# Plain x for the last layer's experts, a gate per token on VectorE, and a new order of all engines

## The reference, cut to what matters

```
logits = xf @ gate_w.T                        # n x 8
w, sel = top_k(logits, 2); w = softmax(w)
w_full = zeros(n, 8).at[arange(n)[:, None], sel].add(w)
expert_out = einsum('nc,edc->ned', xf, expert_w)
out = einsum('ne,ned->nd', w_full, expert_out)
x = layernorm(x + out)
```

## Time and profile before

| | |
|---|---|
| median of 3 runs | 1725.61 us (1722.67 to 1727.79) |
| the profiled execution, its own time | 1721.39 us |
| its span, first to last instruction | 1719.6 us |
| TensorE busy | 85% of the span, granted clock 0.958 of full on average |
| VectorE busy | 75% |
| ScalarE busy | 53% |
| GpSimd busy | 51% |
| DMA | 214.26 MB |

### The profile page before, as it was taken

The page is one execution under the profiler, slowest core; times in us unless marked ns, Lnnn a source line. Parts: engine busy times, 40 slices in busy tenths (PEclk is TensorE's granted clock), DMA queues, the critical chain, the costliest instruction groups (busy, mean ns, idle before and its releaser), DMA issues.

```text
span 1719.6 us, 36166 instructions
## 1 busy us (share of the span) xinstructions
PE 1465.4 (85%) x12928; PEld 1134.0 (66%) x12928; DVE 1297.0 (75%) x3466; ACT 913.0 (53%) x1868; POOL 882.3 (51%) x772
## 2 busy tenths in 40 slices
PE   2799889999999999999999999999999999985534
PEld 1567666776777767777777767677777767664423
DVE  2466888888888888788888888888888888875552
ACT  1356555566655555566655555566565556563310
POOL 0013565555556665555556665555555655555532
PEclk8799999999999999999999999999999999998765
DMA  4223344444444434544444334444444334433330
GB/s 120 98 93 95 113 131 126 152 144 131 138 132 134 128 115 138 152 148 128 139 136 132 126 114 139 152 130 146 124 147 125 119 126 145 148 87 108 83 111 31
DMA packets 88983, 214.26 MB, mean 125 GB/s; under 512 B 10499, under 2 KB 67075, under 8 KB 67459
## 3 DMA queue, kind: packets, MB, share of 16 engines
q1 hardware_dynamic: 88804, 211.95, 40.9%
HBM read 185.97 MB, written 25.69 MB: 123 GB/s over the span
## 4 chain that ended last, share of the span: by engine, by line
PE 39%; DVE 24%; issue 18%; POOL 11%; ACT 3%; DMA 3%; SPq 1%; DVEq 0%; POOLq 0%; ACTq 0%
POOL wb L1059 8%; PE b L508 7%; PE bPV L529 6%; DVE mx L993 5%; PE bS L546 4%; PE b L567 4%; PE bTU L558 4%; PE bTU L559 3%; POOL prod L1068 2%; DVE wb L962 2%; DVE wb L911 2%; PE bS L549 2%; DVE mneg L1036 2%; DVE gat L975 1%; DVE wb L969 1%
## 5 line engine op out<-in xcount | busy, mean ns | idle before, releaser
L1059 POOL TENSOR_TENSOR wb<-wb 128x1024 f32<-128x1024 f32 x64 | 150.6, 2354 | 498.0 <-DVE wb L911 498.0
L993 DVE TENSOR_REDUCE mx<-bS 128x2 f32<-128x512 f32 x512 | 338.5, 683 | 57.2 <-PE bS L549 55.7
L1068 POOL TENSOR_TENSOR prod<-kC,qC 128x512 f32<-128x512 f32 x256 | 349.1, 1399 | 37.2 <-ACT kC L670 37.2
L701 ACT ACTIVATE P<-bTU 128x512 f32<-128x512 f32 x512 | 277.0, 607 | 106.0 <-PE bTU L481 79.1
L1093 POOL TENSOR_TENSOR h<-ub,gBcb 128x256 f32<-128x256 f32 x256 | 184.0, 730 | 188.1 <-DVE ub L1006 153.5
L546 PE MATMUL bS<-stack 96*128 96x256 bf16 x1024 | 217.8, 280 | 35.3 <-DVE mx L993 14.8
L478 PE MATMUL bTU<-stack 97*128 97x256 bf16 x1024 | 227.3, 275 | 5.5 <-ACT P L701 2.5
L481 PE MATMUL bTU<-dist,identh 128*128 128x128 f16 x1024 | 206.5, 220 | 0.0
L558 PE MATMUL bTU<-x1T,w 128*128 128x256 f32 x576 | 184.1, 402 | 24.6 <-DVE h L1006 24.6
L549 PE MATMUL bS<-dist,identh 128*128 128x128 f16 x1024 | 197.1, 223 | 0.0
L710 ACT ACTIVATE sil<-bTU,b 128x256 f32<-128x256 f32 x288 | 130.1, 475 | 104.6 <-PE bTU L559 56.4
(11 more groups left out here) (159 smaller groups left out, 2781.7 us busy)
## 6 DMA issues: line engine op xcount, KB each, us to landing
wb<-d_w SPq DMA_DIRECT2D x64, 1024.0 KB, 7.8
stack<-d_parts SPq DMA_DIRECT2D x192, 192.0 KB
gBcb<-d_cB SPq DMA_DIRECT2D x32, 1024.0 KB, 4.8
gDcb<-d_cD SPq DMA_DIRECT2D x32, 1024.0 KB, 4.7
d_parts<-parts SPq DMA_DIRECT2D x96, 128.0 KB, 5.2
d_w<-wT SPq DMA_DIRECT2D x32, 256.0 KB, 2.1
xT<-in_xT SPq DMA_DIRECT2D x32, 128.0 KB, 4.7
x<-in_x SPq DMA_DIRECT2D x32, 128.0 KB, 2.1
```

Of the source, the lines that this page charges most:

```text
L701: act_f(P[k % 8][:].rearrange("p a b -> p (a b)"), bTU[turn_bank("ST", k)][:], ACT.Exp).then_inc(actA2.done("exp", k), 1)
L993: v.tensor_reduce(mx[:, :, k], bS[k % 2][:].rearrange("p (a b) -> p a b", a=TT), op=ALU.max, axis=AX.X).then_inc(dveA1.done("max", k), 1)
L1059: tt_(pv[:, 8 * n:8 * n + 4, :], pv[:, 8 * n:8 * n + 4, :], pv[:, 8 * n + 4:8 * n + 8, :], ALU.add).then_inc(poolC2.done("add", n), 1)
L1068: tt_(prod[:, 2 * p:2 * p + 2, :], shifted(kC, p), qC[:].unsqueeze(1).to_broadcast([128, 2, T]), ALU.mult).then_inc(poolC1.done("prod", p), 1)
```

## The change

Six things change together.

1. Stage D. TensorE multiplies the plain x of 128 tokens with two experts' weights side by side (256 columns) into a bank of the three that ST and `ab` use in turn: `D.y`, four steps. VectorE adds each expert's output, times the token's gate as a scalar of its partition, to x: `D.acc`, 16 instructions of 128x128 that read PSUM and SBUF. `D.xs`, `D2.y`, `D2.res`, the transpose, copy, store and broadcast of D's gates go. `D2.mom` keeps the moments of the norm.
2. The maxima are written negated in bf16 by the reduction itself; `M.neg` goes.
3. Ranks: a difference and a comparison with a table of the smallest number replace two comparisons, a product and an add.
4. Roots: two steps of a tuned iteration (seven instructions) in place of three (nine).
5. Distances: q is divided by its head's slope and the exponential multiplies by it, so that one fp16 table holds the plain distances of every head; the second product of odd heads in ST goes, and the constant shrinks from 1024 KB to one head's 32 KB.
6. All five orders are new.

```diff
 ORDER = {
     "pe": """
-        A1.qk A1.v B2.z D2.y.0 A2.ST.0 D2.y.1 A2.ST.1 A2.ST.2 A2.ST.3 A2.ST.4 A2.ST.5 A2.ST.6 A2.PV.0 A2.ST.7
-        A2.ST.8 B.xT A2.ST.9 A2.PV.1 D.xT B.lg D.lg A2.ST.10 A2.ST.11 A2.ST.12 A2.ST.13 A2.PV.2 C1.xT A2.ST.14 B.cT
-        A2.ST.15 B.ab.0 A2.PV.3 C1.qk A1.S.0 A1.S.1 B.ab.1 A3.pT A1.S.2 C1.vg B.ab.2 A1.S.3 A1.S.4 B.ab.3 A1.S.5
-        D.cT B.ab.4 A1.S.6 A3.aT C2.out A1.S.7 A1.S.8 B.ab.5 A3.out A1.S.9 A1.S.10 C1.sc A1.S.11 A1.S.12 C1.scT
-        B.ab.6 A1.S.13 A1.S.14 B.ab.7 B.z A1.S.15 C1.wT B.ab.8 M.mT""",
+        A1.qk B2.z A1.v A2.ST.0 A2.ST.1 A2.ST.2 A2.ST.3 A2.ST.4 A2.ST.5 A2.PV.0 A2.ST.6 A2.ST.7 B.xT A2.ST.8 A2.ST.9
+        A2.PV.1 A2.ST.10 C1.xT A2.ST.11 D.xT A2.ST.12 B.lg D.lg A2.ST.13 A2.ST.14 C1.qk A2.ST.15 A2.PV.2 D.y.0 D.y.1
+        A2.PV.3 D.y.2 B.cT C1.vg B.ab.0 A1.S.0 A1.S.1 B.ab.1 A3.pT A1.S.2 A1.S.3 B.ab.2 A1.S.4 A1.S.5 B.ab.3 A1.S.6
+        A1.S.7 C2.out B.ab.4 A1.S.8 A1.S.9 C1.sc A1.S.10 B.ab.5 C1.scT A1.S.11 B.ab.6 B.ab.7 A1.S.12 B.z A1.S.13
+        C1.wT A1.S.14 A3.aT A1.S.15 B.ab.8 A3.out M.mT D.y.3""",
     "act": """
-        A1.qk A2.exp.0 A2.exp.1 A2.exp.2 A2.exp.3 A2.exp.4 A2.exp.5 A2.exp.6 A3n.nm A2.exp.7 C2n.nm B.xT B2.nm D.xT
-        A2.exp.8 A2.exp.9 D2.nm A2.exp.10 A2.exp.11 A2.exp.12 G.ge A2.exp.13 C1.xT A2.exp.14 A2.exp.15 B.cT C1.qk
-        A3.cp B.ab.0 B.ab.1 C1.vg D.cT B.ab.2 B.ab.3 B.ab.4 A3.aT C1.sc B.ab.5 B.ab.6 C1.exp B.ab.7 C1.wT B.ab.8
-        M.mT""",
+        A1.qk A2.exp.0 A2.exp.1 A2.exp.2 A2.exp.3 A2.exp.4 A3n.nm B2.nm A2.exp.5 A2.exp.6 A2.exp.7 A2.exp.8 A2.exp.9
+        B.xT C2n.nm A2.exp.10 D.xT C1.xT A2.exp.11 A2.exp.12 A2.exp.13 G.ge A2.exp.14 D2.nm C1.qk A2.exp.15 B.cT
+        A3.cp B.ab.0 B.ab.1 B.ab.2 C1.vg B.ab.3 B.ab.4 C1.sc B.ab.5 C1.exp B.ab.6 C1.wT A3.aT B.ab.7 M.mT B.ab.8""",
     "dve": """
-        A1.rest A1.v A1.mid A1.lo B2.res D2.res N.root.0 N.root.1 N.root.2 N.root.3 C2.pv.0 C2.pv.1 C2.pv.2 C2.pv.3
-        G.rank C2.pv.4 G.weigh C2.pv.5 C2.pv.6 C2.pv.7 C2.add.0 A1.max.0 A1.max.1 C2.add.1 A1.max.2 C2.add.2 A3.rec
-        B.wu.0 C2.gt A1.max.3 B.wu.1 A1.max.4 A3.num A1.max.5 A1.max.6 B.wu.2 A1.max.7 A1.max.8 C2.res A1.max.9
-        B.wu.3 A1.max.10 B.wu.4 A1.max.11 A1.max.12 C1.mx B.wu.5 B.wu.6 A1.max.13 A1.max.14 C1.sum B.wu.7 A1.max.15
-        M.neg A3.res B.wu.8""",
+        B2.res D2.mom A1.rest N.root.0 A1.v N.root.1 A1.mid N.root.2 A1.lo N.root.3 C2.pv.0 C2.pv.1 C2.pv.2 C2.pv.3
+        C2.pv.4 C2.pv.5 C2.pv.6 G.rank C2.pv.7 G.weigh D.acc.0 C2.add.0 D.acc.1 C2.add.1 A1.max.0 A1.max.1 C2.add.2
+        D.acc.2 B.wu.0 A1.max.2 A1.max.3 C2.gt A1.max.4 A1.max.5 B.wu.1 A1.max.6 A1.max.7 C2.res B.wu.2 A1.max.8
+        B.wu.3 A1.max.9 B.wu.4 A1.max.10 C1.mx A3.rec B.wu.5 A1.max.11 A1.max.12 C1.sum A3.num A1.max.13 A1.max.14
+        B.wu.6 A1.max.15 B.wu.7 A3.res B.wu.8 D.acc.3""",
     "pool": """
-        C2.add.0 C2.add.1 C1.prod.0 C1.prod.1 C1.prod.2 C1.prod.3 C1.prod.4 C1.prod.5 C1.prod.6 C1.prod.7 B.h.1
-        B.h.2 B.h.3 A3.xbo B.h.4 D.xs.0 B.h.5 B.h.6 D.xs.1 B.h.7 D.xs.2 B.h.8 C2.xb D.xs.3""",
+        C2.add.0 C2.add.1 C1.prod.0 C1.prod.1 C1.prod.2 C1.prod.3 C1.prod.4 C1.prod.5 C1.prod.6 C1.prod.7 C2.xb
+        B.h.1 A3.xbo B.h.2 B.h.3 B.h.4 B.h.5 B.h.6 B.h.7 B.h.8""",
     "sp": """
-        A1.part.0 A1.part.1 A1.part.2 C2.wb A1.rows.0 A1.rows.1 A1.rows.2 B.cT B.cb X.xT D.cT A3.x D.cb C1.dw M.m
-        C1.wb D2.out""",
+        C2.wb A1.part.0 A1.part.1 A1.part.2 A1.rows.0 A1.rows.1 A1.rows.2 B.cT A3.x X.xT B.cb D2.out C1.dw M.m C1.wb""",
 }
...
+                    if what == "D.y" and (e := r["D"]) is not None:
...
+                        take(turn_bank(".y", n), ("D", dveD, "acc", 4 * n + 3), t)
+                        o = bTU[turn_bank(".y", n)]
+                        pe.wait_ge(actD.sem, actD.count(e, "xT"))
+                        for tt in range(TT):
+                            i = mm(o[:, tt * T:tt * T + T], x3T[:, tt * 128:tt * 128 + 128],
+                                   ew[:, 2 * n:2 * n + 2, :].rearrange("p x c -> p (x c)"), start=True, stop=True)
+                        i.then_inc(peD.done("y", n), 1)
...
-                            last_part = h % 2 == 0
-                            i = mm(o[:, c], identh[:], dist[:, h, 0, :], start=False, stop=last_part)
-                            if not last_part:
-                                i = mm(o[:, c], identh[:], dist[:, h, 1, :], start=False, stop=True)
+                            i = mm(o[:, c], identh[:], dist[:], start=False, stop=True)
...
+                    if what == "D.acc" and (e := r["D"]) is not None:
+
+                        dve.wait_ge(peD.sem, peD.count(e, "y", n))
+                        if n == 0:
+                            dve.wait_ge(dveG.sem, dveG.count(t - LAG["G"], "c"))
+                            dve.wait_ge(actNC.sem, actNC.count(e, "nm", 1))
+                            dve.wait_ge(actND.sem, actND.count(e - 1, "nm", 1))
+                        o = bTU[turn_bank(".y", n)]
+                        for i in range(4):
+                            x, tt = 2 * n + i // 2, i % 2
+                            if x > 0:
+                                dve.wait_ge(dveD.sem, dveD.count(e, "acc", 4 * n + i - 2))
+                            c = tt * T + i // 2 * 128
+                            v.scalar_tensor_tensor(nD["y"][:, tt, :], o[:, c:c + 128], gc[:, 1, tt, x:x + 1],
+                                                   x3[:, tt, :] if x == 0 else nD["y"][:, tt, :], ALU.mult,
+                                                   ALU.add).then_inc(dveD.done("acc", 4 * n + i), 1)
...
-                        v.tensor_reduce(mx[:, :, k], bS[k % 2][:].rearrange("p (a b) -> p a b", a=TT), op=ALU.max,
-                                        axis=AX.X).then_inc(dveA1.done("max", k), 1)
+                        v.tensor_reduce(mneg[:, :, k], bS[k % 2][:].rearrange("p (a b) -> p a b", a=TT), op=ALU.max,
+                                        axis=AX.X, negate=True).then_inc(dveA1.done("max", k), 1)
...
-                v.tensor_tensor(o[1], lj, li, ALU.is_equal).then_inc(dveG.done("eq"), 1)
-                dve.wait_ge(dveG.sem, dveG.count(e, "eq"))
-                v.tensor_tensor(geq[:, m], geq[:, m], tri[:].unsqueeze(1).to_broadcast([128, n, TT * E * E]),
-                                ALU.mult).then_inc(dveG.done("eqt"), 1)
-                dve.wait_ge(dveG.sem, dveG.count(e, "eqt"))
-                v.tensor_tensor(ggt[:, m], ggt[:, m], geq[:, m], ALU.add).then_inc(dveG.done("add"), 1)
...
+                v.tensor_tensor(ggt[:, m], gdf[:, m], least[:].unsqueeze(1).to_broadcast([128, n, TT * E * E]),
+                                ALU.is_gt).then_inc(dveG.done("gt"), 1)
```

More of the change, by code:

```diff
@@ L500, in one @@
                         i.then_inc(pePV.done("PV", rr), 1)
-                    if what == "D2.y" and (e := r["D2"]) is not None:
-                        tt = n
-                        if tt == 0:
-                            take(6, ("D2", dveDn, "res", 0), t)
-                        for x in range(E):
-                            if tt == 0 and x % 2 == 0:
-                                pe.wait_ge(poolD.sem, poolD.count(e, "xs", x // 2))
-                            i = mm(b6[:, tt * 128:tt * 128 + 128], xs[:, x, tt * 128:tt * 128 + 128], ew[:, x, :],
-                                   start=(x == 0), stop=(x == E - 1))
-                        i.then_inc(peD.done("y", tt), 1)
                     if what in ("B.z", "B2.z") and (e := r[what[:-2]]) is not None:
@@ L548, in one @@
                             c = slice(qt * T + qt * 128, qt * T + qt * 128 + 128)
-                            i = mm(o[:, c], identh[:], dist[:, h, 0, :], start=False, stop=True)
+                            i = mm(o[:, c], identh[:], dist[:], start=False, stop=True)
                         i.then_inc(peA1.done("S", k), 1)
@@ L613, in one @@
                         take(7, ("M", actM, "mT", 0), t)
-                        pe.wait_ge(dveM.sem, dveM.count(e, "neg"))
+                        pe.wait_ge(dveA1.sem, dveA1.count(e, "max", 15))
                         o = b7[:].bitcast(BF)
@@ L789, in moments @@
             def moments(s, e, nb):
-                dve.wait_ge(s.sem, s.count(e, "res"))
                 for tt in range(TT):
@@ L1032, in one @@
                                         ALU.mult).then_inc(dveC1.done("w"), 1)
-                    if what == "M.neg" and (e := r["M"]) is not None:
-                        dve.wait_ge(dveA1.sem, dveA1.count(e, "max", 15))
-                        dve.wait_ge(peM.sem, peM.count(e - 1, "mT"))
-                        v.tensor_scalar(mneg[:], mx[:], -1.0, None, ALU.mult).then_inc(dveM.done("neg"), 1)
             passes(one)
@@ L1113, in bf16 @@
         return u.astype(np.uint16), (u << 16).view(np.float32)
-    def three(a):
-        out, left = [], np.asarray(a, np.float64)
-        for _ in range(3):
-            bits, val = bf16(left.astype(np.float32))
```

(22 more changed lines are left out.)

178 lines of the change are left out of this document (82 added, 96 removed).

## The result

The changed kernel takes 1674.59 us (median of 4 runs, 1669.7 to 1676.99) against 1725.61: ratio 0.9707, 95% interval 0.9688 to 0.9725. Forecast were 1660 and a range of 1625 to 1705. The profiled execution took 1676.99 us, its span is 1675.2.

A forecast was written before the change was run, and what follows sets the result against it. A pass was taken as bound by a relay of engines, not a busy share. Passes 26 x 1.3 = 34, start 2 and tail 35 make 71 us off 1721.4: 1650, 1655 as median, called 1660; range 1625 to 1705.

The forecast's parts named there:

- the likeliest case: Whole kernel: as walked, a pass loses 0.6 to 2 us, giving 1635 to 1685; chance 0.60.
- the walk: One new pass followed in steps between sixteenth maxima: end at 47.0 us against 48.5, with every handoff ideal.
- step (d): To the fourth maximum and `gt`: same steps, two acc (1.9) more, A3.rec (0.3) less; 31.1 us against 33.0.
- the bound of 1.3: VectorE's acc: the prediction is wrong if a four of them takes over 1.3 us; 0.95 expected.
- The second rival: Each acc paid in full, or new waits eat the pass: 48.5 us kept, 1690, up to 1715; chance 0.22.
- the places of TensorE's steps: Between maxima and roots: D2.y (3.9 us a pass) leaves the stretch, only D.y.3 (0.9) stands there.
- 35 forecast: Tail saving in us: 13 after the last gates, 5 in the pass before, 17 in the four before it.
- 13 forecast: After the last gates: four acc steps, 4.3 us, replace VectorE's 17.1 us stand; D2.res and two root steps go.
- No wait for `wb`: Profile after the change: neither `wb` nor the stack would be waited for.
- in each pass: Sign that the prediction is wrong: S.0 or pv.0 waits for a DMA in each pass.
- The wait for the logits: Before the gates: VectorE waits about 2.5 us for the logits in spite of seven pv.
- The slower rival: S waits for its stack, whose stores stand behind 2 MB of wb loads; 1755 with 3.5 us; chance 0.08.

The follow-up runs named there:

- experiment 8: Changed kernel with VectorE's C2.add.0 ahead of D.acc.0 and GpSimd's prod.0 held back until it is done: 1672.12 us, ratio 0.9687.
- Experiment 4: Changed kernel with six more TensorE products of 512 columns a pass, results unread, at its two idle places: 1660.69 us, ratio 0.9641.
- experiment 7: Changed kernel with only the first 4 of the 16 acc of a pass, six experts missing from the sum: 1661.23 us, ratio 0.9627.
- experiment 10: Changed kernel with each of the 16 acc of a pass done twice, the twin into a scratch tile: 1804.12 us, ratio 1.0443.
- experiment 3: Changed kernel with the gates' last product (G.weigh) ahead of C2.pv.7 on VectorE: 1710.0 us, ratio 0.9906.
- Experiment 1: Kernel before with only the new maxima, ranks, roots and distances, keeping the old D path and old orders: 1657.78 us, ratio 0.9606.
- experiment 5: Changed kernel with D2.mom ahead of B2.res on VectorE: 1650.81 us, ratio 0.9578.
- experiment 12: Changed kernel with D2.mom ahead of B2.res and the second half of wb issued behind the store of A1.part.0: 1651.45 us, ratio 0.9574.
- experiment 6: Changed kernel with the second half of wb (C2.wb) issued behind A1.part.0 instead of ahead of it: 1672.19 us, ratio 0.9689.
- experiment 9: Version of experiment 5 with the first half of wb issued ahead of the row of maxima (M.m): 1773.22 us, ratio 1.0276.

## Why the prediction was right, and where its sum was off

**The total.** Forecast 1660, measured 1674.6, within the range and in the direction of the likeliest case. Part of that is luck. The passes gave half of their term and the tail three quarters. And the gain came from another place than the walk gave it to: the small edits bring more than the whole, and the move of D, which gave the change its name, costs time in each pass (below).

**The passes.** The sum took 1.3 us for each, 34; measured were 17.6. Short passes gave 48.52 - 47.41 = 1.1; they end at 47.4, where the walk had 47.0. These 0.4 are in step (d): the walk had VectorE's first add start after one `prod`, as it does, and at its own 1.2 us, and forgot the next `prod`, which starts 0.09 us before it. The add took 2.17. It didn't cost the full 1.0: with the add back at 1.23 the stretch was no shorter (experiment 8). The greater part, 0.4 us on the average pass or 10 to 12 us, is TensorE's clock, of which the walk said nothing. Experiment 4 showed it as the cause: without the falls the mean pass is 0.40 us shorter.

**`acc`.** Its duration, 0.28 to 0.34 us forecast, is 0.339; its spacing 0.26, not 0.24, so four take 1.11 and not 0.95, still under the bound of 1.3 that the prediction named. The walk priced them at this spacing, and that was the wrong question: of the twelve that experiment 7 took out, eight lie in a stretch that GpSimd's `prod` keep, and four before `B2.res`, where `z` is late anyway. The step that was missed is that work reading PSUM can be free beside GpSimd, and that the adds, which read SBUF twice, then cost less. The second rival, `acc` in full, is therefore excluded for these twelve; `acc.0` was never taken out, and sixteen more are not free (experiment 10).

The Trainium skill, "SBUF — State Buffer", section "Who interferes with whom", says that a VectorE instruction with two SBUF inputs contends with a GpSimd one that reads SBUF, over ports that it calls an exclusive lock, and that one with at most one SBUF input (outside the modes that use two ports) does not. The rows agree on both halves: `c` takes 1.9 us beside an add and 0.19 ahead of it (experiment 3), and four `acc` take 1.11 us beside `prod`, where eight in a row take 2.16 in the last stage with GpSimd idle.

The estimate of 290 ns for each `acc`, which the prediction worked out from the Trainium skill, "VectorE: DVE Perf Modes", section "The TRN2 errata — SBUF-src ops pay a fixed extra latency per instruction", is 0.03 us above the measured spacing of 0.26 and my 0.24 is 0.02 below it. So as a price of VectorE's time it is about right; as a price of the pass it is not, by experiment 7.

**Moving D.** The prediction summed VectorE's work of the whole change to nothing and gave the pass's gain to the places of TensorE's steps. Experiment 1 says otherwise. The four small edits bring 2.0 us a pass with all the old orders, and the move of D costs 1.3 of them. Of these 1.3, experiment 5 returns 0.8: its short passes are 0.6 shorter through the earlier roots, and the mean lies 0.2 above them where it lay 0.4 above. The falls of the clock are gone; in the longer passes that are left `pv.0` waits longest for `wb`, which experiment 12 could not mend. The last 0.5 weren't traced to one cause. In experiment 5, whose waits in eight passes are these, most of what VectorE still waits for is `wb`:

```profile
DVE wb L903 <- DMA wb<-d_w: 23.2, 15, 2.3
DVE mC L1020 <- PE b L565: 2.7, 8, 0.3
DVE mneg L1001 <- PE bS L539: 2.7, 8, 0.3
...
DVE gL L826 <- PE b L439: 0.6, 1, 0.6
```

**The tail.** 35 forecast, 26 measured. The last stage behaves as told; VectorE's timeline at its end in the changed kernel:

```profile
1661.79 0.17 DVE L826 COPY gL<-b 128x16 f32<-128x16 f32 x1 [3.31 <-PE b L439]
...
1664.00 0.61 DVE L941 SCALAR_TENSOR_TENSOR nDy<-bTU,gc,x 128x128 f32<-128x128 f32 x2
...
1666.97 2.16 DVE L941 SCALAR_TENSOR_TENSOR nDy<-bTU,gc,nDy 128x128 f32<-128x128 f32 x8 [0.45 <-PE bTU L466]
...
1671.88 0.16 DVE L815 SCALAR_TENSOR_TENSOR n_b<-n_mv,n_r 128x2 f32<-128x2 f32 x1
```

From the end of `c` to the last root step's start it is 8.0 us (1663.90 to 1671.88), where before it was 20.6, by these two lines:

```profile
1695.44 0.17 DVE L872 TENSOR_TENSOR gc<-gw,grec 128x16 f32<-128x16 f32 x1
...
1716.25 0.16 DVE L821 SCALAR_TENSOR_TENSOR n_b<-n_mv,n_r 128x2 f32<-128x2 f32 x1
```

So 12.7 are saved, against 13 forecast. The missing 9 us are earlier. In the last four passes `pv.0` waits 0.8, 0.8, 2.3 and 4.2 us for `wb`, 8.1 in sum, where before it waited 1.1; but with a quarter of the `acc` these waits sum to 12.2 while the tail is 9.8 us shorter, so they are not simply lost time. What the missing 9 us are stays open. "No wait for `wb`" was wrong: `pv.4` waits for the second half in each pass (1.3 us or more), and `pv.0` for the first in about half of those in the middle and in all of the tail. The prediction named such a wait of `pv.0` "in each pass" as a sign that it is wrong; it came half true. The wait for the logits, for which it had 2.5 us, is at most 0.7 in the short passes, behind that for `wb`, and none in the pass shown. In the middle the wait for `wb` mostly hides behind the logits (experiment 6).

**The slower rival.** S waited for its stack twice in the first 240 us (4.4 us in all) and never after that, though both loads of `wb` stood before the stores. But the queue's order has the force that this rival gave it, at another entry: experiment 9 puts 1 MB before a row of the stack and costs 122 us.

## What to carry to other kernels

Take a change apart before trusting its sum: here four small edits were worth 68 us, and the large one with its new orders gave 17 back. Ask of each VectorE instruction beside GpSimd how many inputs it takes from SBUF; one that reads PSUM can be free there, and removing twelve of sixteen gained 0.2 us a pass. Read the granted clock and the idle place before a late instruction, not only who waits, and keep small transfers that something waits for ahead of large ones in the queue.
